# Four triangle-multiplication layers on one core: three normalized buffers, second-half moments on GpSimd, the weight fold one contraction earlier, layer 2's statistics from accumulators

## The chip, the cores and the metric

One core of a Trainium2 chip runs the whole program. The metric is the device time of one execution in microseconds; lower is better. The engines are named as in the profile: PE is TensorE (PEld its weight loads), DVE VectorE, ACT ScalarE, POOL GpSimd, SP SyncE, whose queue issues nearly all the DMAs.

## The reference, cut to what matters

`x` is (1, 256, 256, 64), float32. Four layers of the same form are applied, each with a residual; layer 0 computes its contraction in bfloat16, layers 1 to 3 in float32.

```python
for layer in (L0, L1, L2, L3):
    y = group_norm(x, 32 groups over positions and 2 channels)
    xn = layernorm(y over channels) * w + b
    left  = (xn @ Wl + bl) * sigmoid(xn @ Wlg + blg)   # * mask in layers 0 and 2
    right = (xn @ Wr + br) * sigmoid(xn @ Wrg + brg)   # * mask in layers 0 and 2
    out = einsum('bikh,bjkh->bijh', left, right)       # or over the first spatial axis
    # layers 0 and 1: the output gate before the output projection
    x = x + (layernorm(out) * sigmoid(xn @ Wog + bog)) @ Wo + bo
    # layers 2 and 3: the output gate after it
    x = x + sigmoid(xn @ Wog + bog) * (layernorm(out) @ Wo + bo)
```

The group norm of a layer needs sums over all positions of `x`, that is, over everything that the layer before wrote.

## The kernel before, in words

Every layer runs the same stages, one after the other, each written as five instruction streams that meet at semaphores. `prepare` (L519) turns the sums of the last layer into the group norm's scale. `norm` (L575) streams `x`, normalizes it over channels and stores it as two float16 halves. `project` (L705) makes half of the channels of left and right in SBUF. `contract` (L896) multiplies them over the contracted axis in 16 parts of 4 channels and stores the result in DRAM (OS). `project` and `contract_kept` (L980) do the same for the other 32 channels, whose result stays in SBUF. `finish` (L1147) is the output side.

In both contractions PE makes a part in one of three PSUM tiles, ACT copies it out (L927, L1021) and squares it (L933, L1026), and DVE adds the part to `sum1` (L950, L1056) and its square to `sum2` (L958, L1064), four additions of 128 x 512 elements a part. These sums over channels, of each position, are the moments of the output layernorm. They exist for two halves of the positions, `ut` 0 and 1. `moments` (L1102) is six DVE instructions of 256 columns that make mean and variance out of the sums of a half, `root` (L1118) two ACT instructions that make 1/sqrt. The first half's are made inside `contract_kept` (parts 9 and 12), the second half's inside `finish` at tile `SECOND` = 10 (L1304, L1381), with two loads of ACT's function table around them.

`fold` (L327) multiplies the norm weights of the next layer into its projection weights, scales them and splits them into `whigh` and `wlow`, of which there is one pair. Its pieces are put between parts 1 and 10 of `contract_kept`; each piece waits for the one before on another engine. The parameters of the next layer are loaded by SP at the start of that stage (L1071).

`finish` handles 16 chunks of 2048 columns, each as four tiles of 512. `unrolled` (L260) writes each engine's order out: at step k an engine runs every one of its stages for tile k minus the stage's lag. In layers 0 and 1 (`gate_first`) a chunk goes through these steps.

- DVE, at step 4c: subtract the mean from both halves of the chunk (`normalize_chunk`, L1136; two instructions, L1142 and L1143) into one of two buffers `nrm`. It first waits until PE has turned all of chunk c - 2, which had the same buffer (L1345), and until POOL has finished chunk c - 1 (L1349).
- POOL: multiply the chunk by 1/sqrt in place (L1321).
- PE, tile t at step t: transpose (`turn`, L1233), gate projection (`out_gate`, L1245), and at a lag of 3 the output projection (L1252).
- ACT, tile t: scale and shift (L1273), sigmoid (L1282), at a lag of 7 the square of the new `x` with its sum by the accumulator (L1297).
- DVE, at a lag of 7: gate (L1356); at a lag of 9: add to `x` with its sum by the accumulator (L1363).

PE's turn of tile t needs DVE's gate of tile t - 4, and its output projection of tile t - 3 needs DVE's gate of that tile and its addition for tile t - 5. In layers 2 and 3 DVE's two instructions multiply by 1/sqrt and POOL has no pass; ACT copies (L1277), DVE gates behind the output projection at a lag of 6 (`gate_late`, L1371) and POOL adds to `x` (L1330). Layer 2 then takes statistics of `x` by 64 `bn_stats` on DVE (L1377) and `prepare` aggregates them (L560). Layer 3 turns the result back on PE and ACT (L1259, L1289) and stores it.

SP's order in `finish` is one loop over chunks: load OS of chunk c + 4 when DVE has normalized chunk c, the halves of xn (`xh`) when PE has projected the gate, store chunk c - 1, and load `x` of chunk c + 2 when the store of chunk c - 2 has landed. Each wait holds up everything behind it.

Of the kernel before, what the change touches and what calls it, by code (L numbers as in the profile page):

```python
# [48 lines left out]
P = 128  # L49
# [54 lines left out]
def build(nc, x_in, masks, consts, params, out):  # L104
    ctx = ExitStack()
    with ctx:
# [50 lines left out]
        whigh = sb("whigh", [P, 320], F16)  # L157
        wlow = sb("wlow", [P, 320], F16)
# [168 lines left out]
        def fold(number):  # L327
# [4 lines left out]
            prm, vec, wog, unscale = prms[number % 2], vector_of(number), wogs[number % 2], unscales[number % 2]  # L332
            wout_c, bias_c, late = wout_cs[number % 2], bias_cs[number % 2], not LAYERS[number]["gate_first"]
# [185 lines left out]
        def prepare(number, layer):  # L519
# [3 lines left out]
            from_sums = number > 0 and LAYERS[number - 1]["gate_first"]  # L523
            total, squared_total = small[:, 8:9], small[:, 9:10]
            with nc.Block() as block:
# [18 lines left out]
                def _(dve):  # L544
                    if from_sums:
# [5 lines left out]
                        dve.tensor_scalar(mean, total, 1.0 / TOKENS, None, ALU.mult).then_inc(step.s, 1)  # L551
                        dve.tensor_scalar(dev, total, 1.0 / TOKENS, shift, ALU.mult, ALU.add).then_inc(summed_up.s, 1)
# [152 lines left out]
        def project(block, number, layer, half):  # L705
# [4 lines left out]
            k_is_b, masked = layer["k_is_b"], layer["masked"]  # L710
            dest = LRb if layer["low"] else LR
# [133 lines left out]
        class Homes:  # L845


            def __init__(self, number):
                layer = LAYERS[number]
                low, end, gate_first = layer["low"], number == len(LAYERS) - 1, layer["gate_first"]  # L850
                if low:
                    self.os = [slot(10).bitcast(BF16)[:, i * 1024:(i + 1) * 1024] for i in range(4)]
                    nrm, xh, xt = (11, 12), (13, 0, 1, 2), (14, 15, 3, 6)
                else:
                    self.os = [slot(c)[:, i * 1024:(i + 1) * 1024] for c in (4, 10) for i in range(2)]
                    nrm = (5, 6)
                    xh, xt = ((8, 9, 11, 15), (12, 13, 14, 7)) if gate_first else \
                        ((8, 9), (12, 13)) if end else ((8, 9, 11), (12, 13, 14, 7))
# [37 lines left out]
        def contract(block, number, layer):  # L896
# [7 lines left out]
            parts = [(piece, g) for piece in range(4) for g in range(4)]  # L904
            @block.tensor
            def _(pe):
                pe.wait_ge(products_ready.s, products_ready.n)
                for e, (piece, g) in enumerate(parts):
                    ut, cq = divmod(piece, 2)
                    if e >= 3:  # L910
# [10 lines left out]
            def _(act):  # L921
                for e, (piece, g) in enumerate(parts):
                    if piece >= 2 and g == 0:
# [14 lines left out]
            def _(dve):  # L938
# [3 lines left out]
                dve.wait_ge(sums_cleared.s, sums_cleared.n + 2)  # L942
                for e, (piece, g) in enumerate(parts):
                    ut = piece // 2
                    for two in range(2):
# [17 lines left out]
            def _(sp):  # L963
                for piece in range(4):
# [13 lines left out]
                    (sums_cleared, 2))  # L978

        def contract_kept(block, number, layer):  # L980
# [7 lines left out]
            more = number + 1 < len(LAYERS)  # L988
            if more:
                fold_project, fold_turn, fold_spread, fold_act, fold_start, fold_copy, fold_greatest, fold_row, fold_rest = \  # L990
                    fold(number + 1)
            @block.tensor
            def _(pe):
                pe.wait_ge(products_ready.s, products_ready.n)
                for e, (ut, g) in enumerate(parts):
                    if more and e == 4:
                        fold_project(pe)
                    if more and e == 7:
                        fold_turn(pe)
                    if more and e == 9:  # L1000
                        fold_spread(pe)
# [10 lines left out]
            def _(act):  # L1012
                act.preload_act_table_set("natural_log_exp_and_others")
                for e, (ut, g) in enumerate(parts):
                    if more and e == 6:
                        fold_act(act)
                    if e == 12:
                        root(act, 0)
# [11 lines left out]
            def _(dve):  # L1030
                dve.memset(epso[:, :], EPS * layer["div"] ** 2)
                if more:
                    dve.wait_ge(prep.s, prep.n + (32 if LAYERS[number + 1]["masked"] else 16))
                for e, (ut, g) in enumerate(parts):
                    if more and e == 1:
                        fold_start(dve)
                    if more and e == 4:
                        fold_copy(dve)
                    if more and e == 6:
                        fold_greatest(dve)  # L1040
# [455 lines left out]
```

## Time and profile before

| | |
|---|---|
| runs, median (lowest, highest) | 2288.97 us (2287.56, 2293.33) |
| the profiled execution | 2284.94 us |
| its span | 2283.1 us |
| mean granted clock of PE | 0.951 |
| PE, PEld busy | 86%, 61% |
| DVE, ACT, POOL busy | 79%, 73%, 27% |
| DMA, mean over the span | 248 GB/s |

The span is what the trace covers, the profiled execution's own time is 1.84 us longer. Busy shares are averages over stages with different limits; the granted clock is a share of 2.4 GHz.

### The profile page before, as it was taken

The numbers are of one execution on the slowest core, as the hardware profiler recorded it, in microseconds if no ns is written. First come the engines' busy times: TensorE is split into PE (matmuls) and PEld (weight loads), VectorE is DVE, ScalarE is ACT, GpSimd is POOL, SyncE is SP. The second block draws the span as 40 slices with busy tenths as digits, with TensorE's granted clock in tenths as the row PEclk, the third lists the DMA queues.
The fourth block names the chain that finished last, engine by engine and source line by source line (L and its number), as shares of the span: only waits on it lengthen the run. The fifth ranks groups of instructions, "written<-read, shape, count | busy, mean of one in ns | idle before, by whom it ended". The sixth has DMA issues, their size and how long they took to land. (4 is left out here: it accounts for less than half of the span.)

```text
span 2283.1 us, 46772 instructions
## 1 busy us (share of the span) xinstructions
PE 1971.4 (86%) x13892; PEld 1401.3 (61%) x13892; DVE 1796.7 (79%) x2995; ACT 1663.7 (73%) x2613; POOL 616.1 (27%) x564
## 2 busy tenths in 40 slices
PE   4599878758889898978889989898998979989898
PEld 4433768535533698964543388897553349888565
DVE  5678899978858887867857887787996879786765
ACT  2388788768878776847878876685665878685666
POOL 0100737354310000024430073370563000000465
PEclk8799989879999999999999999999998999999999
DMA  8778939269779847456967893854897986573698
GB/s 327 318 241 263 293 106 286 83 237 368 287 221 279 293 146 253 164 193 249 396 245 243 258 293 96 252 142 175 326 418 230 282 286 199 185 258 111 229 389 303
DMA packets 450420, 566.25 MB, mean 248 GB/s; under 512 B 15216, under 2 KB 346992, under 8 KB 433904
## 3 DMA queue, kind: packets, MB, share of 16 engines
q1 hardware_dynamic: 447984, 547.89, 72.4%
q10 hardware_dynamic: 2304, 16.78, 1.8%
q8 instruction: 62, 1.02, 0.2%
q14 instruction: 70, 0.57, 0.1%
HBM read 384.25 MB, written 180.36 MB: 247 GB/s over the span
## 5 line engine op out<-in xcount | busy, mean ns | idle before, releaser
L758 PE MATMUL bank<-whigh,kept 128*128 128x128 f16 x4096 | 506.1, 227 | 68.2 <-DMA kept<-XH 34.7
L758 PEld LDWEIGHTS bank<-whigh,kept 128*128 128x128 f16 x4096 | 466.0, 125 | 75.0 <-issue 59.2
L758 PE MATMUL bank<-wlow,kept 128*128 128x128 f16 x4096 | 505.3, 227 | 0.0
L758 PEld LDWEIGHTS bank<-wlow,kept 128*128 128x128 f16 x4096 | 466.4, 125 | 0.0
L1330 POOL TENSOR_TENSOR LR<-LR 128x512 f32<-128x512 f32 x128 | 179.5, 1414 | 555.8 <-DVE LR L1371 530.1
L1321 POOL TENSOR_TENSOR LR<-LR,sum 128x2048 f32<-128x2048 f32 x32 | 159.3, 4978 | 554.5 <-DVE LR L1143 554.5
L780 ACT ACTIVATE sigs<-bank,small 128x256 f32<-128x256 f32 x512 | 237.3, 475 | 69.9 <-PE bank L758 62.8
L624 PE MATMUL bank<-LR,cen 128*128 128x512 f32 x512 | 256.3, 626 | 23.8 <-DMA LR<-XT 11.7
L680 DVE SCALAR_TENSOR_TENSOR LR<-bank,small,LR 126x1024 f32<-126x1024 f32 x128 | 164.4, 1284 | 122.4 <-ACT LR L657 122.0
L780 ACT ACTIVATE squares<-bank,small 128x256 f32<-128x256 f32 x512 | 237.0, 474 | 11.5 <-PE bank L758 4.1
L632 PE MATMUL bank<-LR,kst 128*128 128x512 f32 x512 | 240.9, 593 | 5.2 <-ACT LR L653 5.2
L1233 PEld LDWEIGHTS bank<-kst,LR 128*128 128x128 f32 x1024 | 151.7, 193 | 136.3 <-issue 119.8
L795 POOL TENSOR_TENSOR msgs<-sigs,mask_sb 128x256 f32<-128x256 f32 x192 | 127.7, 680 | 376.2 <-ACT sigs L780 371.6
L823 DVE SCALAR_TENSOR_TENSOR LR<-bank,small,squares 128x256 f32 x512 | 222.6, 477 | 1.6 <-ACT squares L780 0.7
L1245 PE MATMUL bank<-LR,wog 128*128 128x512 f16 x768 | 212.3, 386 | 2.6 <-ACT squares L1282 2.6
L915 PE MATMUL bank<-LR 128*128 128x256 f32 (+1 forms) x896 | 189.7, 375 | 16.4 <-ACT kept L927 8.5
L624 PEld LDWEIGHTS bank<-LR,cen 128*128 128x128 f32 x512 | 93.6, 196 | 174.1 <-issue 86.2
L1006 PE MATMUL bank<-LR 128*128 128x256 f32 (+1 forms) x896 | 188.8, 374 | 9.7 <-DVE LR L823 8.0
L1233 PE MATMUL bank<-kst,LR 128*128 128x128 f32 x1024 | 160.3, 280 | 42.0 <-POOL LR L1321 31.7
L915 PEld LDWEIGHTS bank<-LR 128*128 128x128 f32 (+1 forms) x896 | 160.8, 181 | 44.5 <-ACT kept L927 12.3
L653 ACT ACTIVATE LR<-bank,epsx 128x1024 f32<-128x1024 f32 x128 | 142.5, 1113 | 57.4 <-PE bank L632 57.4
L1006 PEld LDWEIGHTS bank<-LR 128*128 128x128 f32 (+1 forms) x896 | 160.2, 180 | 34.9 <-DVE LR L823 8.6
(139 smaller groups left out, 3532.5 us busy)
## 6 DMA issues: line engine op xcount, KB each, us to landing
LR<-XT SPq DMA_DIRECT2D x128, 512.0 KB, 5.2
kept<-XH SPq DMA_DIRECT2D x128, 512.0 KB, 6.3
LR<-XT SPq DMA_DIRECT2D x64, 1024.0 KB, 8.5
kept<-XHA SPq DMA_DIRECT2D x128, 512.0 KB, 4.6
XT<-LR SPq DMA_DIRECT2D x48, 1024.0 KB, 6.3
LR<-XH SPq DMA_DIRECT2D x64, 512.0 KB, 5.9
LR<-XHA SPq DMA_DIRECT2D x64, 512.0 KB, 5.5
OS<-kept SPq DMA_DIRECT2D x12, 2048.0 KB, 7.5
```

Source lines behind the costliest of these rows:

```text
L624: last = pe.matmul(banks[t % 3][:, u * BANK:(u + 1) * BANK], cen[:, :], cols, start=True, stop=True)
L632: last = pe.matmul(banks[3][:, u * BANK:(u + 1) * BANK], K(K_MEAN), sq[t % 2][:, u * BANK:(u + 1) * BANK], start=True, stop=True)
L680: dve.scalar_tensor_tensor(yc[t % 4][0:kept, :], banks[t % 3][0:kept, :], cb[0:kept, :], rs[t % 4][0:kept, :], ALU.add, ALU.mult).then_inc ...
L758: last = pe.matmul(bank(g)[:, j * P:(j + 1) * P], tokens, w[:, half * P:(half + 1) * P], start=part == 0, stop=part == 1)
L780: act.activation(sig[g], bank(g).rearrange("p (m c) -> p c m", m=4)[:, C:, :], ACT.Sigmoid, scale=unscale).then_inc(gates_ready.s, 1)
L823: dve.scalar_tensor_tensor(dest[:, kt, :, bass.ds(m, 4)], bank(g).rearrange("p (m c) -> p c m", m=4)[:, 0:C, :], unscale, gate[g], ALU.mul ...
L915: last = pe.matmul(banks[e % 3][:, c * N:(c + 1) * N], src[:, kt, off_a + ch, ut * P:(ut + 1) * P], src[:, kt, off_b + ch, :], start=kt == ...
L1006: last = pe.matmul(banks[e % 3][:, c * N:(c + 1) * N], src[:, kt, off_a + 4 * g + c, ut * P:(ut + 1) * P], src[:, kt, off_b + 4 * g + c, : ...
L1233: last = pe.transpose(by_token(turn_bank(t))[:, :, j, :], n_t[c % 2][:, :, 4 * q + j], K(K_IDENT))
L1245: last = pe.matmul(bank(2 + t % 2), wog[w][:, :], pair_cols(x, q) if k_is_b else by_b(x, q), start=(w, part) == (0, 0), stop=w == 1)
L1321: pool.tensor_tensor(v, v, token(sum2, c, C), ALU.mult).then_inc(normalized.s, 1)
L1330: pool.tensor_tensor(by_b(x_of(c), q) if end else by_token_cols(x_of(c), q), by_token(gated[t % 4]), by_token_cols(xi[c % len(xi)], q), AL ...
```

## The change

`fold` moves from `contract_kept` to `contract`, pieces and parameter load alike, at the same parts; `whigh` and `wlow` get a second pair. In `finish` of layers 0 and 1 there are three `nrm` buffers, and DVE centers chunk c at step 4(c - 1) in place of 4c. To make room, layer 1 keeps three `xh` buffers in place of four and moves others. The second half's moments go from DVE to POOL as seven instructions, ahead of POOL's pass over chunk 3 (layers 0 and 1) or its addition of tile 6 (layers 2 and 3); `SECOND` becomes 22. Layer 2 loses `bn_stats`: the sum comes from an accumulator on `gate_late`, the sum of squares from ACT's `square`, as in layers 0 and 1. In `contract_kept` the root and the first chunk's normalization come one part earlier.

```diff
-        whigh = sb("whigh", [P, 320], F16)
-        wlow = sb("wlow", [P, 320], F16)
+        halves_of_w = [[sb(f"w{name}{i}", [P, 320], F16) for name in ("high", "low")] for i in range(2)]
...
-            from_sums = number > 0 and LAYERS[number - 1]["gate_first"]
+            from_sums, sum_of_x = number > 0, LAYERS[number - 1]["gate_first"]
...
-                    nrm, xh, xt = (11, 12), (13, 0, 1, 2), (14, 15, 3, 6)
+                    nrm, xh, xt = (11, 12, 7), (13, 0, 1, 2), (14, 15, 3, 6)
...
-                    nrm = (5, 6)
-                    xh, xt = ((8, 9, 11, 15), (12, 13, 14, 7)) if gate_first else \
-                        ((8, 9), (12, 13)) if end else ((8, 9, 11), (12, 13, 14, 7))
+                    nrm, xh, xt = ((9, 6, 15), (8, 5, 11), (12, 13, 14, 7)) if gate_first else \
+                        ((5, 6), (8, 9), (12, 13)) if end else ((5, 6), (8, 9, 11), (12, 13, 14, 7))
...
 # contract: the pieces of fold(number + 1) at e == 1, 4, 6, 7, 8, 9, 10, as they stood in contract_kept
...
 # contract_kept
-                    if e == 12:
+                    if e == 11:
                         root(act, 0)
...
-                    if e == 13:
+                    if e == 12:
                         dve.wait_ge(moment.s, moment.n + (3 if layer["gate_first"] else 8))
                         normalize_chunk(dve, layer, homes, 0)
...
+        def moments_on_gpsimd(pool):
+
+            s1, t1, s2 = sum1[:, 1, 0:N], sum1[:, 1, N:2 * N], sum2[:, 1, 0:N]
+            n = moment.n + 8
+            pool.wait_ge(summed.s, summed.n)
+            pool.tensor_tensor(s1, s1, t1, ALU.add).then_inc(moment.s, 1)
+            pool.tensor_tensor(s2, s2, sum2[:, 1, N:2 * N], ALU.add).then_inc(moment.s, 1)
+            pool.wait_ge(moment.s, n + 1)
+            pool.tensor_scalar(s1, s1, 1.0 / C, None, ALU.mult).then_inc(moment.s, 1)
+            pool.wait_ge(moment.s, n + 2)
+            pool.tensor_scalar(s2, s2, 1.0 / C, None, ALU.mult).then_inc(moment.s, 1)
+            pool.wait_ge(moment.s, n + 3)
+            pool.tensor_tensor(t1, s1, s1, ALU.mult).then_inc(moment.s, 1)
+            pool.wait_ge(moment.s, n + 5)
+            pool.tensor_tensor(s2, s2, t1, ALU.subtract).then_inc(moment.s, 1)
+            pool.wait_ge(moment.s, n + 6)
+            pool.tensor_scalar(s2, s2, 0.0, None, ALU.max).then_inc(moment.s, 1)
...
-            tiles, SECOND = 4 * NCH, 10
+            tiles, SECOND, MOMENTS, AHEAD = 4 * NCH, 22, 9, 4 if gate_first else 0
...
-                unrolled(tiles, (second_root, 0), (scale_shift, 0), (sigmoid, 0), *([(square, SL)] if gate_first else []),
+                unrolled(tiles, (second_root, 0), (scale_shift, 0), (sigmoid, 0), *([] if end else [(square, SL)]),
...
+                def second_moments(k):
+                    if k == (3 if gate_first else 6):
+                        moments_on_gpsimd(pool)
...
                 def normalize(t):
-                    c = t // 4
-                    if t % 4 or t == 0:
+                    c = (t + AHEAD) // 4
+                    if t % 4 or not 0 < c < NCH:
                         return
-                    dve.wait_ge(turned.s, turned.n + t - 4)
-                    if not gate_first or c >= 8:
-                        dve.wait_ge(moment.s, moment.n + (8 if c < 8 else 16))
+                    if c >= len(nrm):
+                        dve.wait_ge(turned.s, turned.n + 4 * (c - len(nrm)) + 4)
+                    if c >= 8:
+                        dve.wait_ge(moment.s, moment.n + 8 + MOMENTS)
                     if gate_first:
                         dve.wait_ge(normalized.s, normalized.n + c)
                     normalize_chunk(dve, layer, homes, c)
...
                     dve.scalar_tensor_tensor(gated[t % 4], bank(4 + t % 2), bias_c, og[t % 4],
-                                             ALU.add, ALU.mult).then_inc(gated_ready.s, 1)
-
-                def count(t):
-                    c, q = divmod(t, 4)
-                    dve.wait_ge(x_ready.s, x_ready.n + t + 1)
-                    dve.bn_stats(stats[:, t, :], pair_cols(x_of(c), q)).then_inc(stats_taken.s, 1)
+                                             ALU.add, ALU.mult,
+                                             accum_out=None if end else stats[:, t, 0:1]).then_inc(gated_ready.s, 1)
```

## Rows read from the trace of the kernel before

**Rows 1.** Windows over stages: length; busy time of each engine; clock, DMA share, GB/s.
```profile
309.00:340.00 31.00, 21.49 (x128) 13.97 (x128) 30.23 (x50) 25.98 (x27) 0.00 (x0) 0.78 0.34 98
...
830.00:887.00 57.00, 55.52 (x256) 48.56 (x256) 41.08 (x64) 32.15 (x31) 0.00 (x0) 1.00 0.43 143
...
953.00:1015.00 62.00, 59.01 (x269) 50.02 (x269) 42.05 (x81) 31.34 (x33) 0.17 (x1) 1.00 0.32 118
...
2112.00:2283.00 171.00, 158.02 (x833) 103.06 (x831) 109.08 (x112) 115.47 (x201) 95.65 (x64) 0.97 0.83 308
```
**Rows 2.** Timeline, layer 0's finish: one steady period on DVE, two tiles on PE.
```profile
596.54 1.22 DVE L1142 TENSOR_TENSOR LR<-LR,sum 128x1024 f32<-128x1024 bf16 x1 [1.64 <-PE bank L1233]
...
605.80 1.23 DVE L1142 TENSOR_TENSOR LR<-LR,sum 128x1024 f32<-128x1024 bf16 x1 [1.64 <-PE bank L1233]
...
615.51 1.02 PE L1252 MATMUL bank<-sigs,prm 128*128 128x512 f32 x2
...
617.47 1.02 PE L1252 MATMUL bank<-sigs,prm 128*128 128x512 f32 x2
```
**Rows 3.** Windows in layer 2's finish, at its start and in the middle.
```profile
1600.00:1616.00 16.00, 13.42 (x60) 7.55 (x60) 15.90 (x22) 10.68 (x16) 7.74 (x7) 1.00 0.75 257
...
1665.00:1682.00 17.00, 16.67 (x74) 9.76 (x75) 16.73 (x22) 10.96 (x17) 10.71 (x9) 1.00 1.02 417
```
**Rows 4.** Timeline, layer 2's finish, one chunk on DVE, and POOL near the end.
```profile
1685.65 1.91 DVE L1142 TENSOR_TENSOR LR<-LR,sum 128x1024 f32<-128x1024 f32 x1
...
1693.87 1.92 DVE L1142 TENSOR_TENSOR LR<-LR,sum 128x1024 f32<-128x1024 f32 x1
...
1709.77 3.48 POOL L1330 TENSOR_TENSOR LR<-LR 128x512 f32<-128x512 f32 x2 [0.97 <-DMA LR<-XT]
```
**Rows 5.** Timeline, layer 1, end of contract_kept and start of finish, DVE and POOL.
```profile
1021.29 0.68 DVE L1064 TENSOR_TENSOR sum<-sum,squares 128x512 f32<-128x512 f32 x1
1026.53 1.23 DVE L1142 TENSOR_TENSOR LR<-LR,sum 128x1024 f32<-128x1024 f32 x1 [4.55 <-POOL LR L1321]
...
1033.60 1.23 DVE L1142 TENSOR_TENSOR LR<-LR,sum 128x1024 f32<-128x1024 f32 x1 [3.14 <-POOL LR L1321]
...
1037.74 3.12 DVE L1107 TENSOR_TENSOR sum<-sum 128x256 f32<-128x256 f32 x1
...
1046.92 1.22 DVE L1142 TENSOR_TENSOR LR<-LR,sum 128x1024 f32<-128x1024 f32 x1 [1.74 <-PE bank L1233]
...
1014.83 11.50 POOL L1321 TENSOR_TENSOR LR<-LR,sum 128x2048 f32<-128x2048 f32 x1 [368.64 <-DVE LR L1143]
...
1036.04 4.53 POOL L1321 TENSOR_TENSOR LR<-LR,sum 128x2048 f32<-128x2048 f32 x1 [2.53 <-DVE LR L1143]
```
**Rows 6.** Timeline, layer 0, the same start of finish, DVE; ACT's root there.
```profile
475.54 1.23 DVE L1142 TENSOR_TENSOR LR<-LR,sum 128x1024 f32<-128x1024 bf16 x1 [4.55 <-POOL LR L1321]
...
494.64 1.22 DVE L1142 TENSOR_TENSOR LR<-LR,sum 128x1024 f32<-128x1024 bf16 x1 [0.46 <-PE bank L1233]
...
503.91 0.42 ACT L1125 ACTIVATE sum<-sum 128x256 f32<-128x256 f32 x1
```
**Rows 7.** Groups of instructions: count, busy us, mean ns, idle before.
```profile
L795 POOL TENSOR_TENSOR squares<-squares,mask_sb 128x256 f32<-128x256 f32 x192 | 125.3, 666 | 7.3 <-ACT squares L780 3.1 <-DVE LR L823 0.6
...
L1377 DVE BATCH_NORM_STATS2 stats<-LR 128x6 f32<-128x512 f32 x64 | 43.4, 680 | 0.2 <-POOL LR L1330 0.2
```
**Rows 8.** Timeline, layer 0, fold on DVE in contract_kept.
```profile
441.08 0.69 DVE L1056 TENSOR_TENSOR sum<-sum,kept 128x512 f32<-128x512 f32 x1 [0.82 <-ACT kept L1021]
...
451.23 0.15 DVE L388 TENSOR_SCALAR small<-bank 128x1 f32<-128x1 f32 x1
...
453.97 0.90 DVE L1056 TENSOR_TENSOR sum<-sum,LR 128x512 f32<-128x512 f32 x1
```
**Rows 9.** Timeline, layer 0's contract: DVE's first addition; SP's next loads.
```profile
311.56 0.69 DVE L950 TENSOR_TENSOR sum<-sum,kept 128x512 f32<-128x512 f32 x1
...
341.48 3.69 SPq L325 DMA_DIRECT2D kept<-XH  x4
```

More of the change, by code:

```diff
@@ L550, in _ @@
                         dve.wait_ge(summed_up.s, summed_up.n + 1)
-                        dve.tensor_scalar(mean, total, 1.0 / TOKENS, None, ALU.mult).then_inc(step.s, 1)
-                        dve.tensor_scalar(dev, total, 1.0 / TOKENS, shift, ALU.mult, ALU.add).then_inc(summed_up.s, 1)
+                        if sum_of_x:
+                            dve.tensor_scalar(mean, total, 1.0 / TOKENS, None, ALU.mult).then_inc(step.s, 1)
+                            dve.tensor_scalar(dev, total, 1.0 / TOKENS, shift, ALU.mult, ALU.add) \
+                                .then_inc(summed_up.s, 1)
+                        else:
+                            dve.tensor_scalar(mean, total, 1.0 / TOKENS, shift, ALU.mult, ALU.subtract) \
+                                .then_inc(step.s, 1)
+                            dve.tensor_scalar(dev, total, 1.0 / TOKENS, None, ALU.mult).then_inc(summed_up.s, 1)
                         dve.wait_ge(summed_up.s, summed_up.n + 3)
@@ L904, in contract @@
             parts = [(piece, g) for piece in range(4) for g in range(4)]
+            more = number + 1 < len(LAYERS)
+            if more:
+                fold_project, fold_turn, fold_spread, fold_act, fold_start, fold_copy, fold_greatest, fold_row, fold_rest = \
+                    fold(number + 1)
             @block.tensor
@@ L909, in _ @@
                     ut, cq = divmod(piece, 2)
+                    if more and e == 4:
+                        fold_project(pe)
+                    if more and e == 7:
+                        fold_turn(pe)
+                    if more and e == 9:
+                        fold_spread(pe)
                     if e >= 3:
@@ L922, in _ @@
                 for e, (piece, g) in enumerate(parts):
+                    if more and e == 6:
+                        fold_act(act)
                     if piece >= 2 and g == 0:
@@ L942, in _ @@
                 dve.wait_ge(sums_cleared.s, sums_cleared.n + 2)
+                if more:
+                    dve.wait_ge(prep.s, prep.n + (32 if LAYERS[number + 1]["masked"] else 16))
                 for e, (piece, g) in enumerate(parts):
                     ut = piece // 2
+                    if more and e == 1:
+                        fold_start(dve)
+                    if more and e == 4:
+                        fold_copy(dve)
+                    if more and e == 6:
+                        fold_greatest(dve)
+                    if more and e == 8:
+                        fold_row(dve)
+                    if more and e == 10:
+                        fold_rest(dve)
                     for two in range(2):
@@ L963, in _ @@
             def _(sp):
+                if more:
+                    load_parameters(sp, number + 1)
                 for piece in range(4):
@@ L1069, in _ @@
             def _(sp):
-                if more:
-                    load_parameters(sp, number + 1)
                 for h in range(2):
```

63 lines of the change are left out of this document (18 added, 45 removed).

## The prediction, made before the changed kernel was run

> **What bounds the kernel now.** I read the windows over stages first, then the waits of each stage, then the timeline of the few periods on which the change acts. No engine binds everywhere, so each edit has to be priced in its own stage.
>
> Layer 0's contraction is DVE's: 30.23 us busy of 31 while PE is at a slow clock, 0.78 of 2.4 GHz. In layers 1 and 2 the same stage is PE's, 55.52 of 57 us, with DVE at 41.08. Layer 3's finish is PE's, 158.02 of 171 us [rows 1].
>
> The finish of layers 0 and 1 is a loop between DVE and PE. One period of four tiles lasts 605.80 - 596.54 = 9.26 us, and in each DVE stands 1.64 us before it may subtract the mean, waiting for PE's turn. PE alone would need 617.47 - 615.51 = 1.96 us a tile, 7.84 a period [rows 2]. There are 1.4 us a period to win, if that wait goes.
>
> Layer 2's finish looks like DVE's: 16.73 us of 17. But in the same window the DMA share is 1.02 at 417 GB/s; at the start of the stage it was 0.75 at 257 [rows 3]. A chunk moves 512 KiB of OS, 1 MiB of `xh`, 1 MiB of `x` in and 1 MiB out, 3.67 MB. DVE's period is 1693.87 - 1685.65 = 8.22 us, and 3.67 MB in 8.22 us would be 446 GB/s, more than moves: the stage lives on loads made ahead, and near its end POOL stands 0.97 us for a load of `x` [rows 4]. At 417 GB/s a chunk takes 8.8 us. The Trainium skill (SBUF — State Buffer, section on the two separate sides) gives about 436 GB/s as the peak of the DMA ports; by that, as an estimate, a chunk could not take less than 8.4 us. The trace stays below that figure.
>
> **The steady periods of layers 0 and 1: nothing.** Before, at step 4k DVE centers chunk k and waits for 4k - 4 turned tiles. After, at step 4k it centers chunk k + 1 and waits for 4(k + 1 - 3) + 4 = 4k - 4. It is the same count at the same step: the third buffer is spent on being a chunk ahead, and none of it is left as slack. The 1.64 us stay, the period stays 9.26 us. What moves is the order at the two ends.
>
> *At the end* step 60 no longer has a chunk to center. That period becomes PE's, 7.84 in place of 9.26 us: -1.4 in each of the two layers, hidden behind nothing, since SP's last store and loads follow DVE's additions.
>
> *At the start* DVE waits for POOL's last pass before each centering, and POOL's pass follows the centering. Let S be the start of chunk 1's centering (1026.53 in layer 1). Before, chunk 2 follows at S + 7.07 (1033.60), POOL's pass over it ends at 1040.57, S + 14.04, and DVE reaches chunk 3 at step 12, S + 20.4 in layer 1 and 494.64 - 475.54 = 19.1 in layer 0 [rows 5, 6]. After, chunk 2 comes at step 4, before any gate; gate 0 at S + 9.4; chunk 3 at step 8 must wait for the same pass, so S + 14.1. Now POOL has its seven moment instructions ahead of chunk 3's pass. A two-input POOL instruction of 256 columns takes 0.67 us [rows 7]; the three with one input have no row, so I bound them by half of that, 0.33 (one of two inputs is read), and by all of it, and take 0.45: 4 x 0.67 + 3 x 0.45 = 4.0, with the waits between them 4.3 us (3.3 to 6). They and chunk 3's centering (2.3 us) exclude each other: DVE's first moment instruction took 3.12 us because it started under POOL's pass and ended with it, 1037.74 + 3.12 = 1040.86, and POOL's first pass took 11.50 us because DVE's additions ran to 1021.97; without them it takes 4.36 [rows 5]. So chunk 3's pass ends at S + 14.0 + 4.3 + 2.3 + 4.5 = S + 25.1, and at step 12 DVE waits for just that: **+6.0 us in layer 0, +4.7 in layer 1**. Queued behind this wait are gates 5 to 8, and PE's output projections behind those. DVE no longer makes the moments itself, and that saving is inside the difference.
>
> The rule of the Trainium skill behind this (SBUF — State Buffer, the two separate sides) is that GpSimd and a VectorE instruction with two SBUF inputs share a port pair that is locked for a whole instruction by whoever starts first. The trace agrees, by the 3.12 and 11.50 us above; without the rule, work given to GpSimd would be free here and the start would cost 2.3 us less.
>
> ACT's root at tile 22 ends about 0.4 us later than chunk 8's centering would start (before, in the same phase: 504.33 against 494.64 + 9.26 = 503.90 [rows 2, 6]): +0.4 a layer. The fourth `xh` buffer of layer 1 costs nothing: layer 2 runs a shorter period with three.
>
> **The fold.** Layers 1 and 2: both contractions are PE's, PE has 269 instructions with the fold and 256 without [rows 1], and it takes its cost along: 0. The parameters come by SP earlier than DVE asks. Layer 0: out of `contract_kept` go 453.97 - 451.23 = 2.74 us for the last piece, nine DVE instructions at 0.3; 5 x 0.3 = 1.5 for the small pieces; and a stall of 0.82 behind it that grows to 1.2 with its square [rows 8]: -5.4. Into `contract` go the same pieces without the contention, 3.7, and since DVE is the bound there, its stalls behind PE's two small fold steps, about 1.5 each (between 0 and 2): +6.8. They shift everything after: SP's loads for the next stage wait for DVE's twelfth part, which ends at 311.56 + 12 x 4 x 0.60 = 340.4, and are issued at 341.48 [rows 9]. Net **+1.4** (-1.2 to +3).
>
> Layer 1's tail gains. There DVE's additions ran to 1021.97 behind PE and ACT, and POOL's pass could only follow them [rows 5]. Without the last fold piece DVE overtakes ACT once (ACT's copy of part 14) and is idle for some 0.8 us; POOL's waiting pass takes the port, DVE's eight additions follow, and chunk 1's centering starts at 1024.3 in place of 1026.53: **-2.2** (-0.8 if POOL doesn't get in). In layer 0 DVE has no such gap. Layer 2's start is ACT's: 0.
>
> **Layer 2's finish.** 64 `bn_stats` of 0.60 us spacing, 38 us, and 2.8 us of moments leave DVE [rows 7]; the accumulator reads cost it nothing by layer 0's spacing. PE would then pace it at 7.84 us, 13 periods x 0.4 + 2.8 + 0.8 = 8.8 us less. The cover is the DMA queue: it is full from the fourth chunk on, and only what is missing at the start can be brought forward. POOL limits that: its additions (4 x 1.31) and DVE's multiplications (2.3) exclude each other, 7.5 us a chunk, and it carries 4.3 us of moments besides. I take **-2.0**, between 0 and -8.8, near the DMA bound. ACT's 64 squares fit: in layer 0 ACT does the same three instructions a tile, and PE's tiles follow each other at 1.96 us [rows 2]. Aggregation in `prepare` becomes two sums, as in layer 1: -1.3.
>
> **Layer 3's finish**: PE's throughout, moments and table loads lie beside it or stall it as before: 0.
>
> **The sum.** Layer 0: +1.4 + 6.0 - 1.4 + 0.4 = +6.4. Layer 1: -2.2 + 4.7 - 1.4 + 0.4 = +1.5. Layer 2: -3.3. Total +4.6 us. The profiled execution took 2284.94 us (span 2283.1 and 1.84 around it) and would take 2289.5; it stands 4.03 below the median of the runs, so the forecast for a median is 2293.6 us. A measurement can tell 0.3% from no change, 6.9 us: 2282.1 to 2295.8 counts as the same.
>
> **The rivals.**
>
> *POOL is too slow for its new work, and the kernel is slower.* Place: the pass over chunk 3 in layers 0 and 1, and tile 6's addition in layer 2. If each of the seven instructions takes about 0.9 us with its wait, the start costs 2 us more in each of layers 0 and 1, POOL's backlog delays layer 2's stores so that nothing is won there (+2), and the colder PE after the longer stand costs 1 us in each: +8, 2302. It decides from 5.5 us for the seven on. For it: POOL is 1.9 times slower than DVE in L1321's kind of work [rows 5]. Against it: 0.67 us for the nearest row.
>
> *DVE's relief in layer 2 is real, and the DMA queue is not at its end.* Then layer 2 gives 8.8 + 1.3, the fold stalls in layer 0 vanish behind PE (-3): 2294 - 7 - 3 = 2284, and 2280 with a quicker start. For it: loads of `x` delayed POOL only at the very end. Against: 446 GB/s needed, 417 seen.
>
> *The third buffer does free the wait*, because the count that I derive is not what holds DVE. Then 13 periods in each of two layers go from 9.26 towards what the DMAs allow: at 417 GB/s, 8.8 in layer 1 and 8.2 in layer 0, so 13 x (0.5 + 1.1) = -21: 2273. The arithmetic of the wait speaks against it.
>
> **How the numbers follow.** My case has 0.52 (own range 2288 to 2299; it reaches past 2295.8, so 0.36 same, 0.16 slower). The slow rival 0.22, all slower. DVE's relief 0.19, half of it below 2282.1. The free wait 0.07, faster. Together: faster 0.17, same 0.45, slower 0.38. The range 2279 to 2304 leaves out the free wait and the outer ends of the others.
>
> **What would show it.** Right: in the finish of layers 0 and 1 the period is still 9.26 us with 1.6 us of DVE waiting for PE's turn; DVE's centering of chunk 4 waits for POOL and starts 25 us after chunk 1's; the last period is 7.8; layer 2's finish shows a DMA share near 1.02 from its first 20 us on, DVE idle, more POOL waits for loads of `x`; layer 0's `contract` has DVE stalls behind ACT's copies. Wrong: a period under 9 us, layer 2's finish shorter by over 6 us, or seven POOL instructions that take over 5.5 us.

## The result and the profile after

The changed kernel takes 2295.3 us (median of 20 runs, 2288.8 to 2301.3), the kernel before 2285.2 us beside it (20 runs, 2279.4 to 2293.3): ratio 1.0042, 95% interval 1.0033 to 1.0052. It is slower by 10 us, more than the 4.6 forecast. The profiled execution took 2291.4 us (span 2289.6, mean clock 0.948), 6.5 longer than that of before.

Windows over stages and over two starts of the changed kernel, columns as in [rows 1]:

```profile
309.00:340.00 31.00, 18.66 (x109) 13.08 (x110) 27.55 (x48) 21.71 (x23) 0.00 (x0) 0.78 0.23 68
836.00:898.00 62.00, 59.01 (x269) 50.01 (x269) 44.21 (x80) 32.20 (x32) 0.00 (x0) 1.00 0.38 129
965.00:1021.00 56.00, 55.12 (x255) 48.55 (x256) 40.07 (x61) 31.12 (x32) 4.13 (x1) 1.00 0.34 129
1609.00:1625.00 16.00, 16.00 (x72) 9.39 (x72) 12.28 (x19) 12.40 (x24) 12.09 (x10) 0.99 0.66 222
1674.00:1691.00 17.00, 15.88 (x72) 9.18 (x71) 13.39 (x19) 15.10 (x32) 11.66 (x8) 1.00 1.02 414
486.00:503.00 17.00, 10.36 (x35) 5.67 (x36) 8.84 (x15) 4.28 (x7) 16.09 (x9) 0.80 0.22 75
494.00:499.00 5.00, 4.14 (x10) 2.29 (x11) 4.04 (x9) 0.75 (x1) 4.67 (x6) 0.50 0.00 2
```

The fold moved from one contraction of layer 1 to the other: `contract` now has the 269 PE instructions and 59.01 us that `contract_kept` had, and `contract_kept` 55.12 us, where `contract` had 55.52 [rows 1]. Layer 2's finish has DVE at 13.39 of 17 us where it was 16.73, and the same DMA share, 1.02 [rows 3]. The last two windows are layer 0's start: PE busy 10.36 us of 17, at a granted clock of 0.80, and inside it 5 us at 0.50, which is 1.2 GHz.

Timeline of layer 0's finish in the changed kernel: the start on DVE, POOL and PE, then two steady centerings, then one last period on PE:

```profile
476.84 1.23 DVE L1166 TENSOR_TENSOR LR<-LR,sum 128x1024 f32<-128x1024 bf16 x1 [4.44 <-issue]
...
490.87 1.67 DVE L1166 TENSOR_TENSOR LR<-LR,sum 128x1024 f32<-128x1024 bf16 x1 [4.08 <-issue]
492.47 1.74 DVE L1167 TENSOR_TENSOR LR<-kept,sum 128x1024 f32<-128x1024 bf16 x1
...
502.87 1.23 DVE L1166 TENSOR_TENSOR LR<-LR,sum 128x1024 f32<-128x1024 bf16 x1 [1.64 <-PE bank L1257]
...
486.27 4.51 POOL L1345 TENSOR_TENSOR LR<-LR,sum 128x2048 f32<-128x2048 f32 x1 [2.47 <-DVE LR L1167]
490.74 0.73 POOL L1113 TENSOR_TENSOR sum<-sum 128x256 f32<-128x256 f32 x1
491.42 1.71 POOL L1114 TENSOR_TENSOR sum<-sum 128x256 f32<-128x256 f32 x1
...
495.00 0.85 POOL L1118 TENSOR_SCALAR sum<-sum 128x256 f32<-128x256 f32 x1
495.93 0.61 POOL L1120 TENSOR_TENSOR sum<-sum 128x256 f32<-128x256 f32 x1
...
498.25 4.52 POOL L1345 TENSOR_TENSOR LR<-LR,sum 128x2048 f32<-128x2048 f32 x1
...
494.86 2.08 PE L1276 MATMUL bank<-sigs,prm 128*128 128x512 f32 x2 [5.80 <-DVE sigs L1385]
...
512.12 1.23 DVE L1166 TENSOR_TENSOR LR<-LR,sum 128x1024 f32<-128x1024 bf16 x1 [1.63 <-PE bank L1257]
...
521.39 1.22 DVE L1166 TENSOR_TENSOR LR<-LR,sum 128x1024 f32<-128x1024 bf16 x1 [1.64 <-PE bank L1257]
...
614.91 1.02 PE L1276 MATMUL bank<-sigs,prm 128*128 128x512 f32 x2
...
622.72 1.02 PE L1276 MATMUL bank<-sigs,prm 128*128 128x512 f32 x2
```

The period is 521.39 - 512.12 = 9.27 us, with the same 1.64 us before the centering as in [rows 2]. The last period is 622.72 - 614.91 = 7.81. At the start DVE stands 4.08 us before chunk 3's centering, until POOL's pass over chunk 2 ends at 486.27 + 4.51 = 490.78; gates are queued behind it, and PE stands 5.80 for them. Chunk 4's centering follows chunk 1's by 502.87 - 476.84 = 26.03 us.

Layer 1's tail, and POOL in layer 2's finish:

```profile
1017.31 5.02 DVE L1075 TENSOR_TENSOR sum<-sum,squares 128x512 f32<-128x512 f32 x1
...
1016.87 4.91 POOL L1345 TENSOR_TENSOR LR<-LR,sum 128x2048 f32<-128x2048 f32 x1 [364.69 <-DVE LR L1167]
```
```profile
1628.91 25.17 POOL L1354 TENSOR_TENSOR LR<-LR 128x512 f32<-128x512 f32 x16
...
1668.39 3.49 POOL L1354 TENSOR_TENSOR LR<-LR 128x512 f32<-128x512 f32 x2 [0.96 <-DMA LR<-XT]
...
1677.17 3.48 POOL L1354 TENSOR_TENSOR LR<-LR 128x512 f32<-128x512 f32 x2 [0.96 <-DMA LR<-XT]
```

POOL does get in here: its pass runs 4.91 us and DVE's addition, begun under it, 5.02. In [rows 5] the pass took 11.50 behind DVE's additions. In layer 2 POOL makes 16 additions without a pause after its moments, which it began at 1621.31, until it has caught up. From then on it waits for a load of `x` in every chunk, 8.78 us apart.

To see where 10 us lie, I cut every trace at four points of each layer: c, PE's first instruction of `contract`; n, chunk 1's centering; t, PE's turn of tile 32; o, its last output projection. The kernels of the experiments below are in the same table (us).

| kernel | L0 c-n, n-t, t-o | L1 c-n, n-t, t-o | L2 c-n, n-o |
|---|---|---|---|
| before | 166.2, 76.0, 76.2 | 196.0, 77.3, 76.2 | 202.9, 132.9 |
| after | 167.6, 83.4, 74.7 | 194.7, 83.4, 74.7 | 203.2, 135.8 |
| accumulators only | 166.8, 77.5, 76.2 | 196.8, 76.0, 76.2 | 202.6, 132.5 |
| moments on DVE | 168.2, 83.0, 74.7 | 194.7, 82.9, 74.7 | 203.3, 134.2 |
| fold in contract_kept | 169.2, 83.4, 74.7 | 195.7, 83.4, 74.7 | 202.6, 133.9 |
| not ahead | 167.4, 71.6, 66.8 | 194.3, 69.5, 66.8 | 202.0, 136.0 |
| not ahead, old wait | 167.2, 72.8, 76.2 | 194.9, 75.7, 76.1 | 203.6, 135.2 |
| two steps ahead | 167.6, 73.8, 66.7 | 194.3, 75.4, 68.5 | 202.0, 135.2 |
| ahead, center last | 166.6, 75.7, 66.8 | 194.4, 75.7, 70.2 | 203.0, 135.7 |
| third buffer alone | 169.3, 70.9, 66.7 | 198.2, 70.9, 68.6 | 201.1, 132.9 |
| third buffer and accumulators | 169.0, 70.9, 66.7 | 198.4, 70.9, 68.1 | 201.2, 133.1 |
| not ahead, POOL's moments in layers 0 and 1 | 167.9, 71.6, 66.8 | 195.2, 69.3, 66.8 | 203.2, 134.5 |
| not ahead, less `xh` in layer 2 | 167.9, 71.6, 66.8 | 194.9, 69.4, 66.8 | 203.2, 130.0 |

One trace of a kernel stands for one execution. How far that goes, the first row and the third show: their first two layers have the same finish, and n-t differs by 1.5 us in layer 0 and by 1.3 the other way in layer 1.

What the change touches adds up to 13 us in this pair of traces: layer 0 +1.4 and +5.9, layer 1 -1.3 and +4.6, layer 2 +0.3, +2.9 and -1.2 in the aggregation. Layer 3 adds -1.0 and +1.7, and I take its +1.7 for scatter: over all traces its finish lies between 155.4 and 157.7 us with the moments on POOL and between 156.0 and 157.3 with them on DVE. Stages that the change leaves alone came out some 7 us shorter in this pair, 4.5 of them in layer 3's `norm` and `project`; those two differ by some 5 us over all traces, so I take it for chance.

### The profile page after: what moved, and what is told of

It is laid out like the page before. It is cut to its first block and busy times, and to the rows that moved or that the text cites. A ratio compares the mean times of both kernels' runs of the same rounds, so it can differ in the third digit from the quotient of the medians.

```text
span 2289.6 us, 46969 instructions
## 1 busy us (share of the span) xinstructions
PE 1977.3 (86%) x13892; PEld 1404.8 (61%) x13892; DVE 1758.7 (77%) x2976; ACT 1704.8 (74%) x2741; POOL 652.1 (28%) x592
## 3 DMA queue, kind: packets, MB, share of 16 engines
q8 instruction: 62, 1.02, 0.2%
## 5 line engine op out<-in xcount | busy, mean ns | idle before, releaser
L1354 POOL TENSOR_TENSOR LR<-LR 128x512 f32<-128x512 f32 x128 | 192.1, 1523 | 521.6 <-DVE LR L1400 492.9
L630 PEld LDWEIGHTS bank<-LR,cen 128*128 128x128 f32 x512 | 93.5, 196 | 172.6 <-issue 83.4
```

The source lines that it names most:

```text
L630: last = pe.matmul(banks[t % 3][:, u * BANK:(u + 1) * BANK], cen[:, :], cols, start=True, stop=True)
L1354: pool.tensor_tensor(by_b(x_of(c), q) if end else by_token_cols(x_of(c), q), by_token(gated[t % 4]), by_token_cols(xi[c % len(xi)], q), AL ...
```

## The experiments

Each ratio is to the kernel before, run on the same chip beside the experiment (medians of 2286.6 to 2288.9 us there); the kernel before had 2285.2 beside the changed kernel, so a difference between medians that were not taken side by side can be off by 3 to 4 us.

**The changed kernel with AHEAD = 0**: three buffers, but no chunk ahead.

```diff
-            tiles, SECOND, MOMENTS, AHEAD = 4 * NCH, 22, 9, 4 if gate_first else 0
+            tiles, SECOND, MOMENTS, AHEAD = 4 * NCH, 22, 9, 0
```

> The changed kernel with AHEAD = 0 in layers 0 and 1: DVE centers chunk c at step 4c as before, with the changed kernel's three buffers, so it waits for 4c - 8 turned tiles where it waited for 4c - 4. Theory A (the third buffer was spent on being a chunk ahead; as slack it frees DVE's 1.64 us): the period goes from 9.26 to what the DMAs allow, about 8.2 in layer 0 and 8.8 in layer 1 (13 periods each: -14 and -6), and the start is some 5 us shorter in each; the last period's 1.4 come back. Program 20 to 28 us faster than the changed kernel, 2267 to 2275. Theory B (the wait moves to POOL's pass over the chunk before or to the output projection): the period stays 9.26, and only the start and the end move, -6 to -8 us.

Measured: 2253.0 us (5 runs, 2252.2 to 2255.3), ratio to the kernel before 0.9848 (0.9829 to 0.9866). That is 42 us faster than the changed kernel by the medians and 44 by the ratios, twice the lower end of what I expected. In layer 1:

```profile
1085.16 1.22 DVE L1166 TENSOR_TENSOR LR<-LR,sum 128x1024 f32<-128x1024 f32 x1
...
1092.95 1.22 DVE L1166 TENSOR_TENSOR LR<-LR,sum 128x1024 f32<-128x1024 f32 x1
```
```profile
1069.00:1101.00 32.00, 31.73 (x146) 19.12 (x145) 30.57 (x59) 32.00 (x66) 18.23 (x4) 1.00 1.02 417
```
```profile
DVE LR L1392 <- DMA LR<-XT: 3.7, 3, 1.9
```

DVE waits for nothing before its centering, and the period is 7.79 us, PE's (31.73 of 32) and by now ACT's too (32.00). The DMA share is 1.02 at 417 GB/s, and I had let that bound layer 1 at 8.8 us a chunk. It does not: 417 GB/s for 7.8 us are 3.25 MB of the chunk's 3.67, so the queue falls behind by 0.42 MB a chunk, and the stage is nearly over before what was loaded ahead is used up. Only in its last 37 us (1110 to 1147) does DVE wait for loads of `x`, three times, 3.7 us in all (the last line: total, times, longest), and the layer's second half still takes 66.8 us like layer 0's.

**That kernel with the old wait put back**: the same buffers and order, another count.

```diff
-                    if c >= len(nrm):
-                        dve.wait_ge(turned.s, turned.n + 4 * (c - len(nrm)) + 4)
+                    if c >= 2:
+                        dve.wait_ge(turned.s, turned.n + 4 * (c - 2) + 4)
```

> The kernel with three buffers and no chunk ahead (AHEAD = 0, 2253 us), and only the wait put back to what it was with two buffers: at step 4c for 4c - 4 turned tiles. Buffers, DMAs and order are the same. Theory A (it is the count in this wait): the period is 9.26 us again with DVE 1.64 us before each centering, and the program 35 to 38 us slower than with 4c - 8, 2288 to 2291. Theory B (the order or the buffers' places matter): it stays under 2270.

Measured: 2281.4 us (10 runs), ratio 0.9970 (0.9956 to 0.9984). A steady centering of layer 0:

```profile
561.92 1.23 DVE L1166 TENSOR_TENSOR LR<-LR,sum 128x1024 f32<-128x1024 bf16 x1 [1.64 <-PE bank L1257]
```

The 1.64 us and the period of 9.26 are back, and 28 us of the 42 with them. My 35 to 38 was too much. Layer 0 shows where: its second half (t-o) is 9.4 us longer with the old wait, its first (n-t) only 1.2, although DVE waits for the count there too. What the free wait would win there, the kernel without it spends on something else, a stand for POOL, whose pass over chunk 3 ends at 502.66 behind the moments:

```profile
502.76 1.23 DVE L1166 TENSOR_TENSOR LR<-LR,sum 128x1024 f32<-128x1024 bf16 x1 [3.43 <-issue]
```

It also has one period of 10.08 us among those of 7.8, the one in which ACT makes the second half's root. The other 14 us lie between this kernel and the changed one. They differ in being ahead alone: n-t is 83.4 against 72.8 in layer 0 and 83.4 against 75.7 in layer 1, and t-o is 1.5 less. Being a chunk ahead costs 10.6 and 7.7 us at the start and gives 1.5 back at the end.

**Moments back on DVE**, in the changed kernel (`SECOND` 10, six instructions, none on POOL).

```diff
-            tiles, SECOND, MOMENTS, AHEAD = 4 * NCH, 22, 9, 4 if gate_first else 0
+            tiles, SECOND, MOMENTS, AHEAD = 4 * NCH, 10, 8, 4 if gate_first else 0
...
+                    unrolled(tiles, (second_moments, 0), (normalize, 0), (gate, GL), (add, AL))
```

> The changed kernel with the second half's moments back on DVE at tile 10 (six instructions), all else as changed. Theory A (POOL's seven instructions, 7.6 us long, hold chunk 3's pass in layers 0 and 1 and the stores in layer 2): chunk 4's centering comes 22 to 23 us after chunk 1's in place of 26.0, so 3 us less in each of layers 0 and 1; layer 2's finish loses its extra 2.9 and perhaps 2 more, layer 3's its extra 1.7; together 9 to 12 us less than the changed kernel, about 2284. Theory B (what is long at the start is being a chunk ahead, and the moments lie beside it): under 3 us less.

Measured: 2291.2 us (12 runs), ratio 1.0013 (1.0000 to 1.0027). In layer 0:

```profile
500.43 3.10 DVE L1131 TENSOR_TENSOR sum<-sum 128x256 f32<-128x256 f32 x1
...
508.31 1.23 DVE L1166 TENSOR_TENSOR LR<-LR,sum 128x1024 f32<-128x1024 bf16 x1 [0.46 <-PE bank L1257]
```

Theory B holds for layers 0 and 1; the program as a whole gives 4 us by the medians and 7 by the ratios, between the two theories. In layer 0 chunk 4's centering comes at 508.31, 26.07 us after chunk 1's at 482.24, where it was 26.03. DVE's moments there are stretched by POOL's pass (3.10 us for the first, 0.41 for the second of the same form) and cost as much as POOL's. Without being ahead, which engine is better is not shown: with the old wait n-t is 72.8 and 75.7 with POOL's moments against 76.0 and 77.3 before (77.5 and 76.0 in the accumulators' run), with the free wait 71.6 and 69.5 against 70.9 and 70.9 in the third buffer alone. In layer 2 the stage is 1.6 us shorter than after.

**Two steps ahead**, and **centering last in the step**: how much slack the wait needs.

```diff
-            tiles, SECOND, MOMENTS, AHEAD = 4 * NCH, 22, 9, 4 if gate_first else 0
+            tiles, SECOND, MOMENTS, AHEAD = 4 * NCH, 22, 9, 2 if gate_first else 0
...
-                    if t % 4 or not 0 < c < NCH:
+                    if (t + AHEAD) % 4 or not 0 < c < NCH:
```

> The changed kernel with AHEAD = 2 in place of 4 in layers 0 and 1: chunk c is centered at step 4c - 2 and waits for 4c - 8 turned tiles, so two of the four tiles of slack are left. Theory A (what counts is slack of more than PE's and ACT's latency of one turn, under a tile and a half): period 7.8 us in both layers, and the start between that of AHEAD 0 and 4: 2253 to 2259. Theory B (each tile of lead costs its share of the 42 us): period 8.5, about 2274.

Measured: 2264.5 us (4 runs), ratio 0.9909 (0.9884 to 0.9934). The period is 7.8 in both layers, as theory A has it, but for the last three of layer 1, 8.45 to 8.78, before which DVE waits 0.6 to 0.7 us for a load of OS. The program missed theory A's range by 5.5 us: layer 1's start takes 75.4 us, as long as with the old wait.

```diff
-                    unrolled(tiles, (normalize, 0), (gate, GL), (add, AL))
+                    unrolled(tiles, (gate, GL), (add, AL), (normalize, 0))
```

> The changed kernel, a chunk ahead and with the wait for 4k - 4 turned tiles at step 4k as it has, with one change of order: in each step DVE gates and adds before it centers. PE may then be one tile further when DVE begins to wait. Theory A (the 1.64 us are the latency of one turn against one tile of slack, and a second tile of slack hides it): the period of layers 0 and 1 falls from 9.26 to 7.8 to 8.1 us, DVE's wait under 0.4 us, and the program is 28 to 40 us faster than the changed kernel, 2256 to 2268. Theory B (only a free buffer helps, the order of DVE within a step moves the wait elsewhere): the period stays over 9 us, and the time within 5 us of 2295.

Measured: 2267.0 us (6 runs), ratio 0.9908 (0.9882 to 0.9934). One line of order in the changed kernel wins 28 us, as theory A has it. Layer 0's second half runs at 7.8 us a period. Layer 1 has a new wait:

```profile
1101.70 1.23 DVE L1166 TENSOR_TENSOR LR<-LR,sum 128x1024 f32<-128x1024 f32 x1 [0.28 <-DMA LR<-OS]
...
1110.43 1.22 DVE L1166 TENSOR_TENSOR LR<-LR,sum 128x1024 f32<-128x1024 f32 x1 [1.11 <-DMA LR<-OS]
```

Who centers a chunk ahead needs OS a chunk earlier, and a DMA queue that is full gives it late: 8.73 us here. So being ahead costs on that side as well once the wait for PE's turn is gone.

**The third buffer alone**, in the kernel before.

```diff
-                    nrm, xh, xt = (11, 12), (13, 0, 1, 2), (14, 15, 3, 6)
+                    nrm, xh, xt = (11, 12, 7), (13, 0, 1, 2), (14, 15, 3, 6)
...
-                    dve.wait_ge(turned.s, turned.n + t - 4)
+                    if c >= len(nrm):
+                        dve.wait_ge(turned.s, turned.n + 4 * (c - len(nrm)) + 4)
```

> The kernel before with one thing of the change, the third nrm buffer in layers 0 and 1 (and the buffer places that go with it, three xh buffers in layer 1), centering of chunk c still at step 4c; the wait is for chunk c - 3 to be turned, 4c - 8 tiles. Moments on DVE, fold in contract_kept, bn_stats. Theory A (the wait for PE's turn is all that stretches the period, and one buffer of slack removes it): period 7.8 us, 13 periods of 1.46 us less in each of two layers, -38 us: about 2250. Theory B (part of the 42 us came from the changed kernel's other parts, moments on POOL above all): -25 us or less, 2263 or more.

Measured: 2254.4 us (4 runs), ratio 0.9853 (0.9826 to 0.9880). The whole gain is in this one part; the rest of the change, without the chunk ahead, adds nothing that these runs can tell.

**The accumulators alone**, and **both parts**.

```diff
-                    unrolled(tiles, (second_moments, 0), (normalize, 0), (gate_late, GL), (count, CL))
+                    unrolled(tiles, (second_moments, 0), (normalize, 0), (gate_late, GL))
...
-                                             ALU.add, ALU.mult).then_inc(gated_ready.s, 1)
+                                             ALU.add, ALU.mult,
+                                             accum_out=None if end else stats[:, t, 0:1]).then_inc(gated_ready.s, 1)
```

> The kernel before with one part of the change: layer 2's statistics by accumulators (the sum on DVE's gate, the square on ACT) in place of 64 bn_stats; moments stay on DVE, two nrm buffers, fold in contract_kept. Theory A (layer 2's finish is held by the DMA queue, and the 2.9 us that it became longer in the changed kernel come from POOL's moments): from chunk 1's centering to the last output projection it takes 131 to 133 us (132.9 before, 135.9 changed), the aggregation gives 1.3, the program is 1 to 3.5 us faster than before. Theory B (the 2.9 us come from ACT's 64 squares or from the accumulator reads): it takes 135 to 136 us here too, and the program is about 1.5 us slower than before. Theory C (DVE's relief is real): 124 us, the program 10 us faster.

Measured: 2285.4 us (12 runs), ratio 0.9983 (0.9971 to 0.9996). POOL's additions in layer 2 there:

```profile
1642.83 3.74 POOL L1336 TENSOR_TENSOR LR<-LR 128x512 f32<-128x512 f32 x3 [1.83 <-DVE LR L1377]
...
1650.84 3.73 POOL L1336 TENSOR_TENSOR LR<-LR 128x512 f32<-128x512 f32 x3 [1.83 <-DVE LR L1377]
```

The period is 8.01 us where it was 8.22 [rows 4], until late in the stage POOL's waits for `x` begin and it becomes 8.78. The stage ends at 132.5 us against 132.9: DVE's relief is used up sooner and nothing more. That is theory A, with 1.2 us of the gain in the aggregation. On top of the third buffer (the run after this one) the stage is 133.1 us against 132.9, so the accumulators give the finish nothing.

> The kernel before with the third nrm buffer as slack and layer 2's accumulators, moments on DVE, fold in contract_kept: the two parts of the change that gained alone. If they add up: the third buffer alone less 3.3 us (what the accumulators alone gave), about 2247. If layer 2's DMA debt does not care (theory that only the first 40 us count): the same 3 us, since both parts are in different layers. If the 2253 us needed the moments on POOL: above 2258.

Measured: 2252.6 us (4 runs), ratio 0.9849 (0.9825 to 0.9872). Against the third buffer alone that is 1.8 us less, inside the scatter; 3.3 can't be told from it.

**The fold back in `contract_kept`**, in the changed kernel (all its pieces and the parameter load, as in the kernel before).

> The changed kernel with the fold and its parameter load back in contract_kept; root and first centering stay one part earlier. Theory A (moving the fold is a zero sum in layers 1 and 2, costs 1.4 us in layer 0, and gains about 2 at layer 1's tail): contract becomes 5 to 6 us shorter in each of layers 0 to 2, contract_kept 4 to 8 longer, the program stays within 2 us of the changed kernel. Theory B (the fold was hidden in contract_kept and is not in contract): contract 5 to 6 us shorter in each of three layers, contract_kept unchanged, the program 15 us faster.

Measured: 2297.4 us (10 runs), ratio 1.0036 (1.0023 to 1.0049), where the changed kernel has 1.0042. `contract` of layer 1 is 55.5 us in place of 61.2 (PE's first to last instruction), and c-n is 169.2, 195.7 and 202.6 against 167.6, 194.7 and 203.2: what one contraction gains the other loses. Layer 2's finish is 1.9 us shorter than in the changed kernel, 133.9 against 135.8, which neither theory had.

**Moments on POOL in layers 0 and 1 only**, not ahead.

```diff
-            tiles, SECOND, MOMENTS, AHEAD = 4 * NCH, 22, 9, 0
+            tiles, AHEAD = 4 * NCH, 0
+            SECOND, MOMENTS = (22, 9) if gate_first else (10, 8)
```

> The kernel with three buffers and no chunk ahead (2253 us), with the second half's moments on POOL in layers 0 and 1 only; in layers 2 and 3 six instructions on DVE at tile 10. Theory A (POOL's moments in layer 2 delay its additions, so the stores, so the loads of x, and the full DMA queue does not make it up): layer 2's finish from chunk 1's centering to the last output projection is 134 us in place of 136.0, layer 3's 156.2 in place of 157.7, the program 2 to 4 us faster, 2249 to 2251. Theory B (those differences were scatter): 2252 to 2254.

Measured: 2255.5 us (5 runs, 2250.9 to 2256.7), ratio 0.9850 (0.9829 to 0.9871). Layer 2's finish is 134.5 us and layer 3's 156.2, as theory A has it (layer 3's lies within its scatter), but the median lies above the range of either theory and is not faster than with all moments on POOL. At this size only the stages can be told apart, not the medians.

**Less `xh` in layer 2**, not ahead. The low half of xn is left out but for an eighth, from chunk 3 on.

```diff
+                if part == 1 and layer is LAYERS[2] and c >= 3:
+                    sp.dma_start(buf[:, 0:256], XH[ut, :, part, :, vb, 0, :]).then_inc(loaded_xh[c % 4].s, 16)
+                    continue
```

> The kernel with three buffers and no chunk ahead, but in layer 2's finish the low half of xn of every chunk from 3 on loads 64 KiB in place of 512 (the rest of that buffer keeps what was there, so part of the gate's input is left out). Same DMA count, 0.46 MB less of 3.67 a chunk. Theory A (the DMA queue holds layer 2's finish): the period late in it falls from 8.78 to PE's 7.8 to 8.0, no more waits of POOL for x, and the stage falls from 136 to 126 to 129 us. Theory B (the share of 1.02 is only occupancy, and ACT or POOL paces the stage): it stays at 134 to 136.

Measured: 2250.8 us (2 runs, 2246.7 and 2255.0), ratio 0.9834 (0.9801 to 0.9866), the stage 130.0 us in place of 136.0, one more than theory A allowed.

```profile
1640.00:1660.00 20.00, 20.00 (x93) 11.90 (x91) 15.20 (x26) 19.12 (x40) 15.58 (x11) 1.00 1.02 415
```
```profile
1646.57 3.74 POOL L1357 TENSOR_TENSOR LR<-LR 128x512 f32<-128x512 f32 x3 [1.84 <-DVE LR L1403]
...
1654.58 3.74 POOL L1357 TENSOR_TENSOR LR<-LR 128x512 f32<-128x512 f32 x3 [1.83 <-DVE LR L1403]
```

The period is 8.01 us to the end and no wait for `x` is left, so the DMA queue cost 6 us of the stage. What paces it then is PE, 20.00 busy of 20, with ACT at 19.12 right behind. The share still reads 1.02: by the share alone one can't tell whether a queue holds the stage; the waits for its loads tell.

## Why the prediction was right in its direction and short by half

The forecast for the median was 2293.6 us and 2295.3 was measured. That the two lie so close is partly luck: the forecast put 4.6 us on a kernel before at 2289.0, and the measurement has 10.1 on one at 2285.2. What the 4.6 was made of came out as follows.

**The steady periods: right.** I counted 4k - 4 turned tiles at step 4k on both sides and said that the third buffer is spent on being ahead. The period is 9.27 and the stand 1.64. The run with 4c - 8 and the run with 4c - 4 on the same buffers show that it is this count. The last period is 7.81 (forecast 7.84), -1.5 us in each layer.

**What the free wait is worth: wrong.** That rival stood at 2273, since I bounded layer 1 by 8.8 us a chunk and layer 0 by 8.2, from 417 GB/s. The kernel that frees the wait takes 2253. Layer 2's own period of 8.22 us, under my bound of 8.8, had shown that loads made ahead carry a stage of 13 periods; I read it so for layer 2 and then forgot it for layers 0 and 1.

**The start of the finish: right in place, short in size, the cause half wrong.** Forecast chunk 4's centering at 25.1 us after chunk 1's, measured 26.03. Forecast +6.4 and +5.1 us until the middle (start and root together), measured 7.4 and 6.1. I put 4.3 us of it down to POOL's seven moment instructions; with the moments on DVE the centering comes at 26.07. It is being ahead that costs 10.6 and 7.7, of which the rest of the change gives 3.2 and 1.6 back (1.6 is hardly more than two traces of the same finish differ by). DVE stands for POOL before the gates it could do, and PE stands 5.80 us behind it and then runs at a granted clock of 0.50 for 5 us. The seven took 7.5 us (490.74 to 498.25) with the centering inside, where I had 4.3 + 2.3: an instruction of one input, bounded at 0.33 to 0.67, takes 0.85.

**The fold: right in its parts, the net in layer 0 not shown.** SP's loads for the next half are issued at 348.39 in place of 341.48 [rows 9], +6.9 for +6.8. From PE's first instruction of `contract_kept` to DVE's last addition there it is 46.6 us in place of 52.0, -5.4 for -5.4 (45.8 to 46.6 against 51.5 to 52.4 over all traces). The net is +1.4 for +1.4 in this pair, but that it came out so is luck: over all traces c-n of layer 0 is 166.6 to 168.2 us with the fold in `contract` and 166.2 to 169.3 with it in `contract_kept`. Layer 1's tail: -1.3 for -2.2, and POOL got in as foreseen; here the traces part cleanly, 194.3 to 195.2 against 195.7 to 198.4.

**Layer 2's finish: this step failed.** Forecast -2.0, measured +2.9. I let DVE's relief bring 2 us forward; it brings nothing that the traces can tell (-0.4 and +0.2 in the two runs with the accumulators and the moments on DVE). Two terms without a price in my sum cost the rest. One is the moments on POOL, which I had only as a limit on what is won. They stand ahead of tile 6's addition and so delay the stores and the loads of `x`: with them on DVE the stage is 1.6 us shorter (135.8 to 134.2), and 1.5 in the kernels that are not ahead (136.0 to 134.5). POOL's first wait for `x` comes 54 to 56 us after chunk 1's centering in every kernel with the moments on POOL and a full load of `xh`, and 79 us or more with them on DVE. My slow rival had this as +2. The other is the fold's place, which I had at 0: with the fold back in `contract_kept` the stage is 1.9 us shorter (135.8 to 133.9), and with the moments on DVE it is 132.5 with the fold there and 134.2 in `contract`. The lower DMA rate at the start of the stage, 222 GB/s where there were 257 [rows 3], goes with the fold and not with POOL, whose moments begin only at 1621.31. Here are the same 16 us, counted from chunk 1's centering, first with the moments on DVE, then with the fold in `contract_kept`:

```profile
1611.70:1627.70 16.00, 13.96 (x63) 7.84 (x61) 15.15 (x21) 11.81 (x21) 8.85 (x6) 1.00 0.68 234
...
1617.50:1633.50 16.00, 16.00 (x74) 9.41 (x73) 12.39 (x21) 13.41 (x27) 13.51 (x11) 1.00 0.76 264
```

From the start of `contract` on, c-o is 334.0 to 336.5 us in the kernels with the fold in `contract_kept` and 337.2 to 339.1 in those with it in `contract` and a full load of `xh`. About one microsecond of that is there when SP issues the first loads; why the fold's place costs the rest is open. The aggregation gave 1.2 for 1.3.

**The sum.** Start +2.0, layer 1's tail +0.9, layer 2 +5.3, layer 3's scatter +0.7 more than forecast: 13 in the trace's stages, 10 in the medians, where I had 4.6. The Trainium skill (SBUF — State Buffer, on the two separate sides) has a DVE instruction with two SBUF inputs and a POOL instruction lock each other out, each for the whole of the other. The trace agrees: 5.02 us for DVE's addition under POOL's pass, and 1.67 and 1.74 us for centerings of 1.22 under POOL's moments.

## What to carry to other kernels

A further buffer helps only as slack in the wait that it was bought for: write out the count waited for at the same step before and after, and if it is the same, nothing is gained. Running ahead in an in-order queue spends the slack and puts the wait in front of work that is ready; with the same three buffers it was the difference between 2295 and 2253 us. Bound a stage by its DMA rate only over more periods than its load buffers can lend, and look for waits on loads, not for a full share.

## What the runs showed of the hardware that I had not expected

- POOL instructions of 256 columns: two inputs 0.61 to 0.73 us, one input (TENSOR_SCALAR) 0.85; 1.71 where DVE's centering ran beside them.
- A DMA share of 1.01 to 1.03 stood for anything from 370 to 425 GB/s, whether the stage waited for loads or not.
- PE's granted clock over the same 17 us of layer 0's start is 0.80 in the changed kernel, where PE stood 5.80 us and was busy 10.36, and 1.00 with AHEAD = 0, where it was busy 15.30. After that stand it is 0.50 (1.2 GHz) for 5 us, and an output projection's pair of matmuls took 2.08 us there against 1.02 in the steady state.
